# A four-layer graph network: roots for ten blocks at once, loops of 20 blocks, and selections kept in DRAM

## The reference

```
for l in range(4):
    m = x @ weight[l]
    agg = segment_sum(m[src], dst, num_segments=n_nodes)
    x = gru_cell(agg, x)     # r, z = sigmoid(...), n = tanh(i_n + r * h_n); (1 - z) * n + z * h
return layernorm(input + (x + input))     # over the 128 features, eps 1e-5
```

## Time and profile before

| what | value |
|---|---|
| median of 3 runs | 2310.44 us (2309.59 to 2311.28) |
| profiled execution | 2312.41 us |
| its span | 2310.7 us |
| PE, PEld busy | 2219.9 us (96%), 1909.5 us (83%) |
| DVE, ACT, POOL busy | 2158.7 us (93%), 1847.9 us (80%), 1660.1 us (72%) |
| chain that ended last | PE 69%, DVE 17%, issue 9% |
| DMA | 362.44 MB, mean 157 GB/s |

### The profile page before, as it was taken

One profiled execution on the slowest core, in us unless ns is written; L12 is line 12 of the kernel. 1 busy time (PEld: TensorE's weight loads), 2 busy tenths in 40 slices (PEclk: granted clock), 3 DMA queues, 4 the chain that ended last, 5 costly groups with the idle time before them and its releaser, 6 DMA issues.

```text
span 2310.7 us, 49242 instructions
## 1 busy us (share of the span) xinstructions
PE 2219.9 (96%) x11764; PEld 1909.5 (83%) x11764; DVE 2158.7 (93%) x4077; ACT 1847.9 (80%) x3483; POOL 1660.1 (72%) x1632
## 2 busy tenths in 40 slices
PE   3999999999999999999999999999989999999996
PEld 2888888888878888888878888888877888888885
DVE  7899999999979999999969999999979999999998
ACT  1688888888858888888857888888856888888887
POOL 3877777777577777777647777777748877777882
PEclk7999999999999999999999999999999999999998
DMA  2455555555545666566645665666553565555564
GB/s 58 114 156 161 160 159 158 161 160 160 152 134 168 172 173 173 171 172 171 171 122 166 174 173 171 172 173 173 172 161 98 158 162 164 160 164 159 164 162 119
DMA packets 277064, 362.44 MB, mean 157 GB/s; under 512 B 107755, under 2 KB 186587, under 8 KB 276981
## 3 DMA queue, kind: packets, MB, share of 16 engines
q1 hardware_dynamic: 238118, 309.12, 45.0%
q0 software_dynamic: 38784, 52.30, 10.2%
q10 hardware_dynamic: 78, 0.08, 0.0%
HBM read 208.71 MB, written 179.20 MB: 168 GB/s over the span
## 4 chain that ended last, share of the span: by engine, by line
PE 69%; DVE 17%; issue 9%; DMA 2%; ACT 1%; POOL 1%; DVEq 1%; POOLq 0%; ACTq 0%; SPq 0%
PE pZ L856 18%; PE pR L856 9%; PE pHN L856 9%; PE pA L844 9%; PE pO L938 5%; PE pA L856 4%; PE pIN L856 4%; PE pR L897 3%; PE pR L900 3%; PE pR L898 3%; DVE narg L1419 3%; DVE diff L1423 2%; DVE bn L1455 2%; DVE aggT L1393 2%; PE pH L787 2%
## 5 line engine op out<-in xcount | busy, mean ns | idle before, releaser
L692 POOL DMA_INDIRECT gath<-state,idx x900 | 942.5, 1047 | 263.7 <-issue 252.3
L675 POOL TENSOR_TENSOR h_lo<-hT,h_hi 128x500 fp32r<-128x500 f32 (+1 forms) x400 | 376.2, 941 | 236.1 <-ACT h_hi L1059 180.9
L692 POOL DMA_INDIRECT gath<-in_x_dram,idx x300 | 322.2, 1074 | 101.9 <-issue 70.1
L1090 ACT ACTIVATE rg<-pR,bsum 128x500 f32<-128x500 f32 x400 | 270.6, 676 | 116.4 <-PE pR L900 103.4
L1412 DVE SCALAR_TENSOR_TENSOR narg<-pHN,bhh,rg 128x500 f32<-128x500 f32 x400 | 292.6, 731 | 47.3 <-ACT rg L1090 45.9
L1071 ACT CAST sel<-sel 128x504 fp32r (+1 forms) x400 | 245.9, 615 | 31.6 <-DVE flag_i L1367 29.5
L1429 DVE TENSOR_TENSOR diff<-pZ,diff 128x500 f32<-128x500 f32 x400 | 268.0, 670 | 0.6
L1384 DVE TENSOR_TENSOR a_lo<-aggT,a_hi 128x500 fp32r<-128x500 f32 x378 | 258.3, 683 | 0.2
L1098 ACT ACTIVATE pZ<-pZ,bsum 128x500 f32<-128x500 f32 x400 | 256.4, 641 | 1.0 <-PE pZ L856 1.0
L1393 DVE TENSOR_TENSOR aggT<-pA,hT 128x500 f32<-128x500 f32 x378 | 252.4, 668 | 2.0 <-PE pA L844 1.8
L1094 ACT ACTIVATE pIN<-narg,bih 128x500 f32<-128x500 f32 x200 | 136.5, 683 | 120.3 <-DVE narg L1419 120.3
(11 more groups left out here) (219 smaller groups left out, 6377.7 us busy)
## 6 DMA issues: line engine op xcount, KB each, us to landing
columns<-newT SPq DMA_DIRECT2D x300, 250.0 KB, 2.3
hT<-columns SPq DMA_DIRECT2D x300, 250.0 KB, 2.8
state<-o_rows SPq DMA_DIRECT2D x300, 224.0 KB
x_rows<-in_x_dram SPq DMA_DIRECT2D x200, 224.0 KB
out_dram<-o_rows SPq DMA_DIRECT2D x91, 224.0 KB
gath<-state,idx POOLq DMA_INDIRECT x900, 2.5
state<-o_rows SPq DMA_DIRECT2D x297, 26.0 KB
idx<-edge_src SPq DMA_DIRECT2D x395, 1.5 KB
```

Of the source, the lines that this page charges most:

```text
L675: nc.gpsimd.tensor_tensor(part_of(h_lo, u)[:, cols], hT[:, u % RING, cols], part_of(h_hi, u)[:, cols].bitcast(F32), ALU.subtract).then_inc ...
L692: pool.indirect_dma_start(out=gath[:, u % RING, j, :], out_offset=None, in_=states[l], in_offset=bass.IndirectOffsetOnAxis(ap=idx[:, u % R ...
L1090: nc.scalar.activation(rg[:, :], pR[:, 0:COLS], ACT.Sigmoid, bias=bsum[:, 0:1]).then_inc(s_r, 1)
```

## The change

- The last layer makes the roots of BATCH = 10 blocks at once (nine such batches, one of five blocks, then the two at the end as before). OUTLAG becomes 13, and y has 20 slots: ten in `y_rows`, ten over the memory of `sel8`.
- `sel8` is thus gone in the last layer. So layer 0 stores each widened selection to DRAM (`store_selection`, after `load_x` in SP's step), with ScalarE waiting for the store before it widens into the same slot again; the last layer loads them (`load_selection`) into five slots that lie over `sel`, `g_hi` and `g_lo`, and widens nothing. The first five loads are issued in layer 2's last step.
- UNROLL is 20, so each layer has 20 straight steps, a loop body of 20 steps that runs three times, and 20 straight steps.
- VectorE's waits for s_HN in `r_times_hn` and, in the last layer, for s_cstore in `new_state` are left out, but for the first block or blocks.
- The own blocks are those with u % 5 == 4.
- In the last 20 steps ScalarE normalises six columns a step from the 13th on (`caught_up`, `rows_by`), and SP stores accordingly.

```
-UNROLL = 10
+UNROLL = 20
+BATCH = 10
+OWN = (4,)
-OUTLAG = 9
+OUTLAG = BATCH + 3
...
+    selections = nc.dram_tensor("selections", [NB, P, SELW], F32, kind="Internal").ap()
...
+        mixed = sb("mixed", [P, max(2 * SELW + 2 * GATHERED, RING * SELW)], F32R)
+        sel = mixed[:, 0:2 * SELW].rearrange("p (t c) -> p t c", t=2)
...
+        sel_loaded = mixed[:, 0:RING * SELW].bitcast(F32).rearrange("p (t c) -> p t c", t=RING)
...
+        y_more = sel8_mem[0:ROWS, 0:4 * BATCH * RPP * D].bitcast(F32).rearrange("p (u c) -> p u c", u=BATCH)
+        def y_slot(u):
+            return y_rows[:, u, :] if u < UNROLL - BATCH else y_more[:, u - (UNROLL - BATCH), :]
...
         def by_tensor(l, b, u):
-            return l == L - 1 and u % RING == 0 and not (isinstance(b, int) and b < UNROLL)
+            return l == L - 1 and u % RING in OWN and not (isinstance(b, int) and b < UNSPLIT)
...
-        def half_done(i, u, at):
+        def batch_done(i, u, lag):
+            first = u - lag - (BATCH - 1)
+            if isinstance(i, int) and i == GROUPS - 1 and first == 2 * BATCH - UNROLL + RING:
+                return slice(UNROLL - BATCH, UNROLL - RING), NB // BATCH - 1
+            if first % BATCH:
                 return None
...
+        def caught_up(i, u):
+            return isinstance(i, int) and i == GROUPS - 1 and u >= BATCH
+        def rows_by(u):
+            behind = RPP * (NB - UNROLL + BATCH - OUTLAG)
+            return behind + max(0, min(u - BATCH + 1, 3)) * RPP + max(0, u - BATCH - 2) * (RPP + 2)
...
+            def store_selection(b, u):
+                sp.wait_ge(s_sel, b + 1)
+                sp.nop(nofuse=True)
+                sp.dma_start(columns_of(selections, b), sel[:, u % 2, :].bitcast(F32)).then_inc(s_selst[u % 2], 16)
+            def load_selection(b, u, summed):
+                sp.wait_ge(s_pA, summed)
+                sp.nop(nofuse=True)
+                sp.dma_start(sel_loaded[:, u % RING, :], columns_of(selections, b)).then_inc(s_selld[u % RING], 16)
...
+                        if l == 0 and exists(i, u, 2):
+                            store_selection(*after(i, u, 2)[:2])
+                        if l == L - 1 and exists(i, u, RING):
+                            load_selection(b + RING, u, l * NB + b + 1)
+                        if l == L - 2 and last:
+                            for c in range(RING):
+                                load_selection(c, c, (l + 1) * NB)
...
-                pe.wait_ge(s_sel, g + 1)
+                if l == L - 1:
+                    pe.wait_ge(s_selld[u % RING], 16 * (turn(i, u) + 1))
+                else:
+                    pe.wait_ge(s_sel, g + 1)
...
-            def widen(l, b, u):
+            def widen(l, b, u, i=0):
                 if l == 0:
                     act.wait_ge(s_sel8, b + 1)
+                    if not isinstance(b, int) or b > 1:
+                        act.wait_ge(s_selst[u % 2], 16 * (UNROLL // 2 * i + u // 2))
                     act.nop(nofuse=True)
...
                     def normal(i, u, part):
-                        if final and exists_before(i, u, lag):
+                        if final and caught_up(i, u):
+                            middle = rows_by(u - 1) + 2
+                            halves = range(rows_by(u - 1), middle, 2) if part == 0 else range(middle, rows_by(u), 2)
+                            for r in halves:
...
-                        if final and not ramp and exists(i, u, 3):
-                            widen(l, *after(i, u, 3)[:2])
...
-            def r_times_hn(l, b, u):
+            def r_times_hn(l, b, u, hn_late=False):
                 g = l * NB + b
-                dve.wait_ge(s_HN, g + 1)
+                if hn_late:
+                    dve.wait_ge(s_HN, g + 1)
                 dve.wait_ge(s_r, g + 1)
...
-                        new_state(l, b, u, (TURNS * l + t if not final else TURNS * l) if again else None,
+                        if final:
+                            stored = TURNS * l if isinstance(b, int) and b < RING else None
+                        else:
+                            stored = TURNS * l + t if again else None
+                        new_state(l, b, u, stored,
                                   g - RING + 1 if again else None)
...
-                        half = half_done(i, u, RING + ROWLAG) if final else None
-                        rooted = half_done(i, u, RING + ROWLAG + 1) if final else None
+                        half = batch_done(i, u, ROWLAG) if final else None
+                        rooted = batch_done(i, u, ROWLAG + 1) if final else None
...
-                        ahead = slice(RING, UNROLL - LATE), TURNS - 1
-                        late = slice(UNROLL - LATE, UNROLL), TURNS
+                        ahead = slice(UNROLL - RING, UNROLL - LATE), NB // BATCH
+                        late = slice(UNROLL - LATE, UNROLL), NB // BATCH + 1
```

More of the change, by code:

```diff
@@ L321, in build @@
         s_sel = sem("selection_widened")
+        s_selst = [sem(f"selection_stored_{u}") for u in range(2)]
+        s_selld = [sem(f"selection_loaded_{u}") for u in range(RING)]
         s_pA = sem("edges_summed")
@@ L518, in fast_path @@
                         indices(c, c)
+                    if l == 0:
+                        for c in range(2):
+                            store_selection(c, c)
                     def step(i, u, first, last):
@@ L549, in step @@
                             load_columns(l, b + RING, u)
-                        if l == L - 1 and exists_before(i, u, OUTLAG):
+                        if l == L - 1 and not caught_up(i, u) and exists_before(i, u, OUTLAG):
                             store(l, *after(i, u, -OUTLAG)[:2])
+                        if l == L - 1 and caught_up(i, u):
+                            for c in range(rows_by(u - 1) // RPP, rows_by(u) // RPP):
+                                store(l, c, c % UNROLL)
+                        if l == 0 and exists(i, u, 2):
[5 more added lines that the diff above has]
+                                load_selection(c, c, (l + 1) * NB)
                         if l < L - 1 and not exists(i, u, RING):
@@ L563, in fast_path @@
                     else:
[L564 to L567, removed]
+                        for c in range(rows_by(UNROLL - 1) // RPP, NB):
+                            if c >= NB - RING:
+                                sp.wait_ge(s_olast, c - (NB - RING) + 1)
+                            store(l, c, c % UNROLL, c * RPP >= rows_by(UNROLL - 1))
                 for u in range(RING):
@@ L1155, in step @@
                         if first:
-                            for c in range(2):
+                            for c in range(0 if final else 2):
                                 widen(l, c, c)
@@ L1191, in step @@
                         normal(i, u, 1)
-                        if ramp and u != 1:
+                        if ramp and u != 1 and not final:
                             widen(l, {0: 2, 2: 5, 3: 6}[u], {0: 2, 2: 5, 3: 6}[u])
@@ L1195, in step @@
                             high_part(l, 5, 5)
[L1196 removed]
+                        if opening(i, u) and not unsplit(l, b + 3):
                             high_gathered(l, *after(i, u, 3)[:2], turn(*after(i, u, 3)[:0:-1]))
                     blocks(act, step)
[L1200 removed]
+                    for r in range(rows_by(UNROLL - 1), NB * RPP, 2) if final else ():
+                        c = r // RPP
+                        if r // RPP * RPP < rows_by(UNROLL - 1):
+                            normalise(c % UNROLL, TURNS * l + c // RING, batch(GROUPS - 1, c % UNROLL) + 1, r % RPP // 2)
+                        elif r % RPP == 0:
+                            normalise_in_place(c % UNROLL, batch(GROUPS - 1, c % UNROLL) + 1,
+                                               RPP // 2 if c >= NB - RING else RPP)
+                    for k in range(0 if final else lag, 0, -1):
                         pb, pu, pi = after(GROUPS, 0, -k)
[L1202 to L1204 removed]
+                        if k > 1:
                             rows_out(l, pb, pu, earlier(turn(pi, pu)))
@@ L1550, in step @@
                             aggregate(l, 4, 4)
-                        r_times_hn(l, b, u)
+                        r_times_hn(l, b, u, first and l == 0)
                         if not ramp and not last:
@@ L1575, in step @@
                         if half:
-                            variance(half[0], RING * (half[1] + 1))
+                            variance(half[0], b - ROWLAG + 1)
                         if rooted:
                             root_second(*rooted, 6)
-                        if not opening(i) and exists(i, u, 3) and not final:
+                        if not opening(i, u) and exists(i, u, 3) and not final:
                             low_gathered(l, *after(i, u, 3)[:2])
@@ L1601, in step @@
                             low_part(l, 5, 5)
-                        if opening(i) and not unsplit(l, b + 3):
```

(1 more changed line is left out.)

95 lines of the change are left out of this document (53 added, 42 removed).

## The result

The changed kernel takes 2317.6 us in the median (2315.61 to 2321.32, eight runs) against 2310.02 for the kernel before: ratio 1.0035, 95% interval 1.0024 to 1.0046. It is slower by some 7.6 us, where I forecast 1.6 less, hardly a change. The time lies inside the range, between the two forms of rival B (2314 and 2319.4).

The account below looks back on a forecast made before the run. TensorE was taken to bound layers 0 to 2, TensorE and VectorE both full in layer 3; -3.7 - 3.4 + 0.5 + 1.5 + 2.7 + 0.8 = -1.6 gave a 2308.8 us median against 2310.44, range 2302 to 2320.

Parts of the forecast that it names:

- rival B: Loop back edges: bodies of twenty blocks no longer held, 2.65 us per refetch; 2314, 2319.4 or 2330 by layers hit; chance 0.26.
- Loops of 20, taken at 0: Back edges, seven to two a layer: each engine's branch runs beside others' work, so 0; bound -20 x 0.056 = -1.1.
- the deciding point: Loop bodies: where one engine's body, VectorE's first, is longer than what is kept; no row showed where it lies.
- Roots, -3.7: Last layer on VectorE: nine fewer root batches, 9 x 0.46 = -4.1, less 0.4 for wider batches; bounds 0 and -8.1.
- The term for wider batches: VectorE's root instructions in the last layer: 125x40 costs as much as 125x20 or a little more, 0.4 us allowed.
- Own blocks, -3.4: First own sum, block 10: moving it later leaves at most 0.8 of a 4.2 us loss waiting for POOL's h_lo.
- +0.5 for layer 0's stores: Layer 0: ScalarE waits for late landings of the stored selections, 0.5 us in all; bounds 0 and 29.
- +1.5 for the boundary: Layer 2 to 3: the first five selection loads go ahead of the last state stores, delaying the first gather; bounds 0 and 3.8.
- Last group, +2.7: Last 20 steps: ScalarE normalises six columns a step, not four, about 0.6 us a step over 4.5 steps; bounds 0 and 4.6.
- Tail, +0.8: After the last loop: 28 columns on ScalarE instead of 26, 2 x 0.385 = +0.8 us; bounds 0 and 0.8.
- Waits left out, 0: VectorE's omitted waits: 0, lying beside executing instructions with TensorE bounding layers 0 to 2; in layer 3 perhaps some tenths.

Follow-up runs that it names:

- the first experiment: The changed kernel with VectorE's steps of the last layer written out straight, other engines as they are: 2309.98 us, ratio 1.0 to the kernel before.
- the second: The changed kernel with SyncE's (SP's) steps straight in all four layers, the others as they are: 2315.2 us, ratio 1.0021 to the kernel before.

## Why the prediction was wrong

**Loops of 20, taken at 0: this step failed.** I counted branches and gave the refetch to rival B. It is what happened: VectorE lost 3.2 and 2.8 us at its two edges of the last layer, close to the 2.65 that SP's last jump showed. VectorE's share (7.6 us by the first experiment, 6.0 of it at the edges) and SP's (2.4 by the second) are the two terms that the sum lacked; without them the kernel takes 2307.07. That this is near the forecast's 2308.8 is luck: 2.2 us of it are SP's last jump, straight code gains in the kernel before as well, and against that kernel without loops the rest of the change, forecast at -1.6, gives nothing. I had VectorE's doubling before me, and could have named the deciding point better by counting the body with its waits. SP's share I missed altogether: I treated a late SP as harmless, as it was before, while the change itself made ScalarE wait for what SP issues. The same step was wrong the other way too: a held back edge isn't free on a full VectorE (0.23 us, seven before).

**Roots, -3.7.** VectorE's work fell: 110.35 to 109.24 in twenty blocks. The time fell by 0.32 there against the kernel before without loops, 1.05 from block 10 to block 90, and by 0.83 against the one with loops of ten. In the changed kernel itself roots of ten are worth 5.3, of which the traces show 3.7 from block 10 to block 90 and the rest in the ten blocks ahead. So the size depends on what own blocks stand beside. With ten, nearly all of VectorE's idle in the twenty blocks is 0.40 us just behind each own block that has no batch beside it, every second one; with five, in the kernel before without loops, it has next to none. The mechanism was right; its number held against this one control alone.
The term for wider batches was too small: from one start to the next a root instruction takes 104 ns in the mean before (125x20) and 129 after (125x40). Over nine batches of ten instructions that is some 2.3 us of VectorE's time, where the sum allowed 0.4.

**Own blocks, -3.4.** The step at the first own block takes 5.86 without any idle:

```profile
1803.20 0.48 PE L922 MATMUL pR<-h_hi,whh_hi 128*128 128x500 f32 x1
...
1806.04 0.39 PE L907 MATMUL pA<-h_hi,ident_r 128*128 128x504 f32 x1
...
1809.06 0.47 PE L922 MATMUL pR<-h_hi,whh_hi 128*128 128x500 f32 x1
```

The stall went as forecast. In time the move is worth some 2.5 in the changed kernel without loops; on the kernel before it is not clear of noise.

**Selections.** +0.5 for layer 0's stores was 2.4, and not by landing late. +1.5 for the boundary: the place was right, the first gather comes 13.45 us after the last rg of layer 2, before 10.14. It comes 12.9 to 13.5 us after it in every trace with the loads ahead of the stores, and 10.1 to 11.1 in those without the loads. But moving the loads brings no time, and by block 10 the traces with and without them overlap (78.4 to 83.6 us and 77.8 to 80.9); what the loads cost in all is open, as no run left them out alone.

**Last group, +2.7.** Measured +2.4 from block 90 to 99. ScalarE's rows, as in the earlier trace rows:

```profile
2265.58 0.66 ACT L1163 ACTIVATE rg<-pR,bsum 128x500 f32<-128x500 f32 x1
...
2269.91 1.64 ACT L1195 ACTIVATE o_rows<-y_rows,nmr,rstd 125x128 f32<-125x128 f32 x4
2271.45 0.65 ACT L1163 ACTIVATE rg<-pR,bsum 128x500 f32<-128x500 f32 x1
...
2274.08 0.68 ACT L1167 ACTIVATE pA<-narg,bih 128x500 f32<-128x500 f32 x1 [0.69 <-DVE narg L1504]
```

Four columns stand between z and rg, for 1.54 us where two took 0.77, and the step is 5.87 (2265.58 to 2271.45). That term held in place, and nearly in size.

**Tail, +0.8.** Behind block 99 the difference shrinks from 7.75 to the spans' 4.8. Some 2.2 of it is SP's last jump, 2.65 us before, which now finds its target held:

```profile
L675 SPq COMPARE_BRANCH  x2: 38/42/45, 61.0 to 2314.8; - x2
```

```profile
L111 SPq DRAIN  x1: 64/64/64, 2315.2 to 2315.2; - x1
```

**Waits left out, 0.** Right: putting them back shows no difference.

On the page of the Trainium skill that spoke against the change ("Runtime: NRT & Kernel Launch", "Instruction fetch mechanics"): that a taken branch to code no longer held stalls its engine agrees with the 3.4 us behind layer 3's branch. The 512 instructions that it gives for most engines, taken in the prediction as the longest body that stays, do not agree: a body of 352 did not stay, and the measurement decides. Whether a body of 352 at another place would stay, no run here shows.

## What to carry to other kernels

Before a loop body is doubled, count each engine's instructions in it, waits and register operations included, and look in the trace for the gap between the loop's branch and the instruction behind it; an engine that is the bound, or that another now waits for, pays for it, 3.2 us of a gap of 3.4 here. An engine that could be late without harm stops being so the moment a change makes someone wait for it. Where two engines are both full, work taken off one is worth only what the other has to spare in the same step, so compare against a control that has everything else alike: here the kernel before without loops, which took away the whole gain that the changed kernel without loops seemed to have.

## What was not expected of the hardware

VectorE's loop bodies of up to 337 instructions were held over the back edge, with some 0.3 us from the branch to the instruction behind it, and bodies of 352 and more were fetched again, with 3.2 to 3.8 us there. VectorE idled 1.9 to 3.2 us at such an edge, sometimes in two gaps. Code without any loop, with each engine fetching all the time, ran no slower than loops: 2306.44 against 2310.22 for the kernel before.
